# A state-space block and spiking layer: three of sixteen accumulations of the last token tile move from GpSimd to VectorE

## What is computed

```python
xz = gn(x) @ W_in                       # 256 -> 2 x 512
xh, z = split(xz)
xc = depthwise_conv3x3(xh)              # 512 channels
dt_r, Bp, Cp = split(xc @ W_xproj)      # 8, 16, 16
dt = softplus(dt_r @ W_dt + b_dt)       # 512 per position
dtN = dt @ W_dtN + b_dtN                # 16 per position
# scan over the 2304 positions of an image, 512 channels x 16 states
h = exp(dt * A) * h + (dtN * Bp) * xc   # A has one value per state
y = sum_over_states(h * Cp) + Dskip * xc
y = layernorm(y) * ln_g + ln_b
x = x + (y * silu(z)) @ W_out + b_out
# second layer, the images are its time steps
v = v + (gn(x) @ W.T + b - v) / 2;  spike = v >= 1;  v = 0 where spike
out = x + spike
```

## Time and profile before

| | us |
|---|---|
| median of three runs | 4952.61 |
| lowest, highest | 4947.26, 4958.85 |
| the profiled execution, its own time | 4945.67 |
| its span, first to last instruction | 4943.9 |
| busy: VectorE (DVE) | 4229.9 |
| busy: GpSimd (POOL) | 4341.3 |
| busy: TensorE, matmuls (PE) | 3728.6 |
| busy: ScalarE (ACT) | 3215.9 |
| mean granted TensorE clock, share of full | 0.894 |

### The profile page before, as it was taken

The page is one execution under the profiler, slowest core; times in us unless marked ns, Lnnn a source line. Parts: engine busy times, 40 slices in busy tenths (PEclk is TensorE's granted clock), DMA queues, the critical chain, the costliest instruction groups (busy, mean ns, idle before and its releaser), DMA issues.

```text
span 4943.9 us, 75444 instructions
## 1 busy us (share of the span) xinstructions
PE 3728.6 (75%) x20244; PEld 2283.6 (46%) x20244; DVE 4229.9 (86%) x4061; ACT 3215.9 (65%) x4722; POOL 4341.3 (88%) x3387
## 2 busy tenths in 40 slices
PE   4777777777777777877877777787777777877865
PEld 1444444444444444544444444444544444444443
DVE  0888888899889988999888988889988899889994
ACT  1666666666766666667666666666666666676662
POOL 1989999989999889989989899998998889999992
PEclk8889998988999889899899889988998988889986
DMA  2222221222122211222122212122222222212210
GB/s 56 85 63 66 66 63 50 80 72 69 47 71 71 72 56 61 68 79 63 60 63 73 65 56 73 59 70 59 74 64 61 59 77 67 63 46 77 69 37 19
DMA packets 189421, 315.34 MB, mean 64 GB/s; under 512 B 51993, under 2 KB 164121, under 8 KB 188961
## 3 DMA queue, kind: packets, MB, share of 16 engines
q1 hardware_dynamic: 188960, 310.06, 21.3%
HBM read 171.87 MB, written 20.05 MB: 39 GB/s over the span
## 4 chain that ended last, share of the span: by engine, by line
POOL 30%; issue 24%; PE 21%; DVE 11%; ACT 7%; SPq 3%; DMA 1%; POOLq 1%; DVEq 1%; ACTq 0%
POOL st L537 20%; PE ht L1063 8%; DVE st L936 6%; PE work L1040 4%; POOL xb L591 3%; SPq L410 3%; POOL dt L628 3%; PE work L1100 2%; DVE y L922 2%; POOL y L582 2%; ACT decay L688 2%; ACT dt L724 1%; ACT xb L756 1%; PE work L1129 1%; ACT dt L757 1%
## 5 line engine op out<-in xcount | busy, mean ns | idle before, releaser
L936 DVE TENSOR_TENSOR_SCAN st<-decay,st 128x1024 f32<-128x1024 f32 (+1 forms) x1536 | 2730.4, 1778 | 347.5 <-POOL st L544 183.3
L537 POOL TENSOR_TENSOR st<-xc,bbc 128x1536 f32<-128x1536 f32 x768 | 2670.9, 3478 | 12.0 <-DMA bbc<-brow 11.3
L688 ACT ACTIVATE decay<-dt,neg_a 128x1024 f32<-128x1024 f32 (+1 forms) x1536 | 1363.2, 901 | 756.5 <-DVE st L936 751.6
L1063 PE MATMUL ht<-ident,st 128*128 128x128 f32 x9216 | 1389.5, 304 | 486.6 <-DVE st L936 466.4
L1063 PEld LDWEIGHTS ht<-ident,st 128*128 128x128 f32 x9216 | 1160.1, 156 | 819.8 <-issue 518.2
L922 DVE SCALAR_TENSOR_TENSOR y<-ht,ct,y 128x512 f32<-128x512 f32 x1536 | 1116.6, 727 | 152.9 <-PE ht L1063 152.5
L582 POOL TENSOR_TENSOR y<-y,weighed 128x512 f32<-128x512 f32 x768 | 992.3, 1292 | 272.1 <-ACT weighed L707 268.5
L707 ACT ACTIVATE weighed<-ht,ct 128x512 f32<-128x512 f32 x768 | 524.9, 683 | 370.1 <-PE ht L1063 363.0
L1040 PE MATMUL work<-tri,conv_w 96*32 96x384 f32 x4608 | 497.3, 572 | 171.4 <-issue 118.8
L1095 PE MATMUL work<-xn,win 128*128 128x384 f32 x768 | 334.8, 579 | 113.6 <-DVE ob L887 64.7
L1090 PE MATMUL work<-xn,win 128*128 128x480 f32 x768 | 364.4, 599 | 5.1 <-ACT xn L803 3.1
(11 more groups left out here) (92 smaller groups left out, 3538.6 us busy)
## 6 DMA issues: line engine op xcount, KB each, us to landing
bbc<-brow SPq DMA_DIRECT2D x192, 768.0 KB, 4.7
tri<-xhp SPq DMA_DIRECT2D x2304, 50.0 KB, 2.0
xin<-in_x_dram SPq DMA_DIRECT2D x48, 384.0 KB, 3.2
out_dram<-ot SPq DMA_DIRECT2D x48, 384.0 KB, 6.6
brow<-xp SPq DMA_DIRECT2D x48, 24.0 KB, 1.5
win<-in_L_conv_W_in_dram SPq DMA_DIRECT2D x1, 1024.0 KB
wo<-in_L_conv_W_out_dram SPq DMA_DIRECT2D x1, 512.0 KB
w1s<-in_L_conv_W_dram SPq DMA_DIRECT2D x1, 256.0 KB, 3.2
```

Source lines behind the costliest of these rows:

```text
L537: u = g.tensor_tensor(slot, xc[:, kq % 2, :, :], bbc[:, piece_slot(kq, p), n % PIECE, :].unsqueeze(1).to_broadcast([P, DC, T]), ALU.mult)
L688: a.activation(flat(decay[:, :, :])[:, lo:hi], flat(dt[:, (k + ahead) % 2, :, :])[:, lo:hi], ACT.Exp, scale=neg_a[:, n:n + 1]).then_inc(s_ ...
L936: v.tensor_tensor_scan(state[:, lo:hi], flat(decay[:, :, :])[:, lo:hi], state[:, lo:hi], 0.0 if h == 0 else state[:, lo - 1:lo], ALU.mult, ...
L1063: last = t.transpose(ht[:, m, c * P:(c + 1) * P], st[:, j, c, m * P:(m + 1) * P], ident[:, :])
```

## The change

`OWN = (8, 10, 11)` names three states. For these, ScalarE no longer weighs the third token tile and GpSimd no longer adds it. VectorE does both in one instruction, of the same form as its other accumulations, behind the two scan parts and two accumulations of the step after. TensorE waits for the right one of the two semaphores before it overwrites bank 2, and the counts of weighings are adapted.

```diff
+OWN = (8, 10, 11,)
+NWT = NS - len(OWN)
...
+        def weighings(q, n):
+
+            return q * NWT + sum(m not in OWN for m in range(n))
...
                 i = (b * K + k - before) * NS + n
+                if n in OWN:
+                    return
                 if n == 0:
                     await_emptied(pool, b, k, "yi2")
                 else:
                     pool.wait_ge(s_y2, i)
-                pool.wait_ge(s_wt, i + 1)
+                pool.wait_ge(s_wt, weighings(b * K + k - before, n + 1))
...
                     if n == 0:
                         await_emptied(act, b, k - 1, "ct")
+                    if n in OWN:
+                        return
                     need(act, s_y2, i - 1)
                     act.wait_ge(s_ht, NT * (i + 1))
...
+            def accumulate_last(b, k, n):
+
+                i = (b * K + k) * NS + n
+                dve.wait_ge(s_ht, NT * (i + 1))
+                dve.wait_ge(s_y2, i)
+                v.scalar_tensor_tensor(out=y[:, k % 2, NTD, :], in0=ht[:, NTD, :],
+                                       scalar=ct[:, k % 2, NTD * NS + n:NTD * NS + n + 1],
+                                       in1=y[:, k % 2, NTD, :], op0=ALU.mult, op1=ALU.add).then_inc(s_y2, 1)
...
+                    if main and s >= Y_LAG and s - Y_LAG in OWN:
+                        accumulate_last(b, k, s - Y_LAG)
...
-                            need(pe, s_wt, i)
+                            past = (n - 1) % NS
+                            if past in OWN:
+                                need(pe, s_y2, i)
+                            else:
+                                need(pe, s_wt, weighings(i // NS if isinstance(i, int) else b * K + k - before, n))
```

## The result

| | before | changed |
|---|---|---|
| median of four runs | 4949.93 us | 4884.01 us |
| lowest, highest | 4946.51, 4958.85 | 4875.24, 4889.57 |
| profiled execution | 4945.67 us | 4875.24 us |
| mean granted TensorE clock | 0.894 | 0.882 |

The ratio is 0.9859, 95% interval 0.9839 to 0.9879: the kernel became faster by 1.4%; the two medians lie 66 us apart. Forecast were 4797 us and a range of 4757 to 4880. The direction was right, the gain less than half of the 155 us forecast.

A forecast was written before the change was run, and what follows sets the result against it. GpSimd was taken to bound steps 9 to 13, VectorE the steps after. Per image 3 x 2.9 + 2 x 3.5 + 3.7 = 19.4 us, times 8 is 155: 4945.67 to 4790, plus 6.9 gives 4797 us; range 4757 to 4880.

The forecast's parts named there:

- Steps 9 and 10, dt addition 1.85 us earlier: GpSimd's dt addition and scan input 11 come 1.85 us earlier; 1.7 taken as gain at scan 11.
- The waits before scans 13 and 14: VectorE's waits of 1.78 and 1.95 us in a tile k = 2 disappear.
- k = 0 and 5: Row tiles with neither charge nor fire gain 3.5 us each.
- Does the gain stay?: After scan 14: GpSimd's phase in the next tile's step 1 is unchanged, nothing lost or won until step 9.
- L903 will meet a gate: Step 11: the fire on VectorE meets a GpSimd gate of 1 us; 0.65 us charged.
- TensorE, 0.6 us: Step 13: TensorE's queue does not fully follow scan 14's earlier start; 0.6 us taken off the 3.5 gain.
- Rival 1: TensorE takes GpSimd's place in steps 12 to 14; about half the last wait stays, 77 us: 4876 us, chance 0.15.
- The bounds: Charge and fire meeting GpSimd: up to 82 us more or 16 less; TensorE: up to 32 us more.
- Rival 3: Moving work between GpSimd and VectorE does not help, VectorE's gain in step 13 is paid back: 4953 us, chance 0.04.

The follow-up runs named there:

- e3: Changed kernel with the second layer's charge and fire replaced by tiny memsets, membrane not computed: 4717.88 us.
- e2: Kernel before the change with the second layer's charge and fire replaced by tiny memsets, membrane not computed: 4880.71 us.
- e5: Changed kernel, GpSimd holding scan input 4 until after the charge and input 5 until after the fire in k = 2, 3, 4: 4814.32 us.
- e13: Changed kernel plus 34 tiny GpSimd memsets behind its layer norm in step 1 of k = 2, 3, 4: 4830.10 us.
- e6: Kernel before the change with only states 10 and 11 moved to VectorE: 4974.05 us, ratio 1.0043.
- e8: As e5, and GpSimd also starts the gates of step 11 only behind the fire in k = 1, 2, 3: 4770.03 us.
- e4: Changed kernel, GpSimd holding scan input 3 until after the charge and input 4 until after the fire in k = 2, 3, 4: 4958.05 us.
- e1: Kernel before the change with only state 8 moved to VectorE: 4866.41 us, ratio 0.9801.
- e10: Changed kernel plus nine tiny GpSimd memsets behind its layer norm in step 1 of k = 2, 3, 4: 4900.80 us.
- e12: Changed kernel plus twenty tiny GpSimd memsets behind its layer norm in step 1 of k = 2, 3, 4: 4898.95 us.
- e11: As e8, with the second layer's output transposes issued in step 14 instead of 13 where the charge is in step 10: 4772.80 us.

## Why the prediction was wrong

The forecast gain was 155 us, the measured one 66. The two terms that went wrong are about equally large: some 48 us in steps 1 to 8, some 42 in steps 9 to 15 and 0.

- **Steps 9 and 10, dt addition 1.85 us earlier: right.** The charge of step 10 shrank from 2.70 to 1.20 us, and steps 9 and 10 of k = 2 became 1.9 us shorter together, where 1.7 was taken.
- **The waits before scans 13 and 14: right.** Idle time ended by GpSimd fell from 220.1 to 61.9 us, and without charge and fire the change gained 163 us (e3 against e2), forecast 155.
- **k = 0 and 5: right, in part by luck.** They gained 3.5 and 4.2 us, forecast 3.5. But with the prediction's own numbers VectorE would reach scan 13 of k = 0 only 1.85 - 0.65 - 0.65 + 1.48 = 2.03 us earlier, not 2.4. The 1.48 of the earlier trace rows is one tile; the mean of the middle images is 1.79.
- **"Does the gain stay?": this is the step that failed.** It said that in step 1 GpSimd waits for VectorE already, so its phase there is as before, and nothing is lost or won until step 9. GpSimd did not wait: its idle time in step 1 was within its own layer-norm chain ("0.20 <-POOL ln_mr L621" above). GpSimd came about 1 us late out of steps 11 to 13 and carried that lateness to step 2. That lateness let the charge start 0.08 us ahead. Rid of two accumulations of 1.27 us behind the dt addition, GpSimd is early, and the charges of k = 2 and 4 and their fires make steps 2 and 3 longer by 2.4 to 3.0 us each, 11.1 us per image. Part of that came back in step 6, where VectorE waits for TensorE's transposes (k = 2: 8.5 us before, 4.7 changed). In sum steps 1 to 8 lost 6.0 us per image instead of 0. e5 and e13 show the cause, e6 that the early leaving of the gates brings it. k = 1 has 2.5 of the 6.0 us: 0.8 is the meeting in its step 1, for the rest (1.3 of it in step 6) no run shows the cause.
- **Term "L903 will meet a gate", 0.65 us: mechanism right, size off.** L913 took 1.05 us, but L916 behind it 1.75 instead of 0.95, because the second gate began between the two. Step 11 of k = 1 to 3 went from 6.4 to 8.3 us, 1.9 more, where 1.3 (0.65 for the added work, 0.65 for the meeting) was forecast.
- **Term "TensorE, 0.6 us": too small.** Step 13 was to gain 1.35 us in k = 1, 2, 3; it changed by -0.4, 0.4 and 0.6. L996 waited 62.3 us for TensorE against 23.9. With the fire and the gates kept apart (e8) the step gains 0.5 to 1.0, so part of this wait followed from the meeting in step 11.
- **Rival 1** (TensorE takes GpSimd's place) is there in this small form. Its own figure of 4876 us lies near the 4884 measured by chance: its mark, L932 waiting longer for transposes, did not appear.
- **The bounds** took the meetings of VectorE and GpSimd to lie in steps 10 and 11 only, where the change is. That their upper end of 82 us is near the 87 us missing (4884 - 4797) is chance too: most of the loss lies elsewhere.
- **Rival 3** (moving work between these two does not help). The added instructions do not meet GpSimd (0.742 us against 0.728 for L932). What meets was there before, and the change shifted its time. That the change doesn't help was wrong; that meetings of the two take a share of the gain was right.

## What to carry to other kernels

Where two engines exclude each other for whole instructions, list all the places where they can meet in the period, not only those beside the change, and read for each the lead of one over the other; a lead as small as the 0.08 us here is luck, and any change of phase can turn it. An engine that comes early is not harmless: make it wait for the other one's instruction where it has time to spare, as e5 and e8 do with one or two waits on a semaphore that was there already. Which of its instructions is held decides: one step too early, in e4, the same wait cost 74 us. And read an idle time that recurs at the same place by its releaser before calling it a point at which the phases are tied.

## What the runs showed that was not expected

- A kernel can get faster by useless work: 34 memsets instead of 20 took 69 us off.
- A charge (two SBUF inputs) that starts while GpSimd makes a scan input lasts 4.24 to 4.30 us less its lag behind that input, in all six traces compared (before, changed, e1, e6, e10, e12); 3.45 of this is the scan input, 0.96 its own work (the two overlap in the records by 0.1 to 0.2 us). A group-norm instruction of two columns waits in the same way: 3.33 us instead of 0.16. When the charge starts first, GpSimd's scan input behind it is longer instead: 4.21 against 3.45 us. The Trainium skill ("SBUF — State Buffer", "Who interferes with whom") has the rule, whoever starts first holds the port for the whole instruction, and these traces agree with it. Two such VectorE instructions in a row, L913 and L916 in step 11, did not hold it through: a GpSimd instruction came in between, and the second took 1.75 us instead of 0.95.
- Removing 212 us of VectorE's work from the kernel before brought 75 us (e2), and removing a wait of 22 us brought nothing (e11). In this kernel part of a local gain in steps 2 and 3 comes back as a longer step 6 of k = 2 to 4: 10.2 of 13.6 us per image in e2, 8.9 of 17.8 in e13 against e12.
